# Moving an expert-weight transpose from TensorE and ScalarE to VectorE and the SP queue

## The reference: one attention layer and one retrieval FFN

```python
x = hidden_states                                   # (8, 2048, 256) float32
# attention: causal linear attention in chunks of 128, mixed with a fixed memory
sq, sk = elu(q) + 1, elu(k) + 1
A   = (sq_i @ sk_i.T) * tril                        # per chunk
out = (A @ v_i + sq_i @ S_kv) / (A.sum(-1) + sq_i @ z);  S_kv += sk_i.T @ v_i;  z += sk_i.sum()
x = x + layernorm((g * memory_output + (1 - g) * out) @ w_o.T)
# FFN: dense part and product-key experts (4 heads, 8 of 1024 experts each)
h = layernorm(x)
scores, indices = top_8(sx[:, None] + sy[None, :])  # two side scores per head, 1024 experts
w = silu((h @ down_embed[indices].T) * softmax(scores))
x = x + layernorm(silu(h @ W_up.T) @ W_down.T + w @ up_embed[indices])
```

## Time and profile before

| | |
|---|---|
| time, median of 3 runs | 3063.93 us (3062.81 to 3065.03) |
| time of the profiled execution | 3065.58 us |
| its span in the profile | 3063.8 us, so 1.8 us lie around it |
| PE busy | 3018.3 us, 99% |
| ACT busy | 2625.7 us, 86% |
| DVE busy | 2174.2 us, 71% |
| POOL busy | 1822.3 us, 59% |
| share of the chain of waits on PE | 96% |
| DMA: software queue (POOL's), hardware queue (SP's) | 36.5% and 4.3% of the 16 engines' span |

### The profile page before, as it was taken

The page is one execution under the profiler, slowest core; times in us unless marked ns, Lnnn a source line. Parts: engine busy times, 40 slices in busy tenths (PEclk is TensorE's granted clock), DMA queues, the critical chain, the costliest instruction groups (busy, mean ns, idle before and its releaser), DMA issues.

```text
span 3063.8 us, 48516 instructions
## 1 busy us (share of the span) xinstructions
PE 3018.3 (99%) x16506; PEld 2460.5 (80%) x16506; DVE 2174.2 (71%) x5644; ACT 2625.7 (86%) x4114; POOL 1822.3 (59%) x2455
## 2 busy tenths in 40 slices
PE   6999999999999999999999999999999999999997
PEld 5788888888888888888888888888888888888886
DVE  4767767776776777777677767767777776777774
ACT  3888888888888888888888888888888888888885
POOL 2665566566556656655665665566566556656653
PEclk8999999999999999999999999999999999999999
DMA  3344344334434433443443344344344434434443
GB/s 91 72 86 80 76 82 83 75 77 86 80 76 81 84 74 77 86 80 76 82 83 74 77 85 80 76 82 84 73 78 85 80 76 82 84 73 78 85 76 71
DMA packets 96201, 244.17 MB, mean 80 GB/s; under 512 B 8659, under 2 KB 46548, under 8 KB 95956
## 3 DMA queue, kind: packets, MB, share of 16 engines
q0 software_dynamic: 53248, 201.34, 36.5%
q1 hardware_dynamic: 42708, 39.73, 4.3%
HBM read 22.94 MB, written 16.78 MB: 13 GB/s over the span
## 4 chain that ended last, share of the span: by engine, by line
PE 96%; DMA 1%; issue 1%; POOL 0%; ACT 0%; SPq 0%; DVE 0%; POOLq 0%; DVEq 0%
PE banks L510 84%; PE banks L559 4%; PE banks L583 2%; PE banks L515 2%; PE banks L545 2%; PE banks L587 2%; PE banks L547 1%; DMA wexp<-wexp 1%; DMA sums<-in_L_ffn_keys_dram 0%; SPq L344 0%; POOL sums L400 0%; PE banks L494 0%; PE banks L501 0%; PE banks L479 0%; POOL rstd L386 0%
## 5 line engine op out<-in xcount | busy, mean ns | idle before, releaser
L400 POOL TENSOR_TENSOR sums<-scores 128x1024 f32<-128x1024 f32 x512 | 1076.7, 2218 | 389.6 <-ACT scores L632 389.6
L510 PEld LDWEIGHTS banks<-xn2T,wupT 128*128 128x128 f32 x4096 | 477.3, 192 | 9.2 <-DVE state L841 2.7
L510 PE MATMUL banks<-deT,xn2T 128*128 128x512 f32 x1024 | 481.3, 592 | 0.0
L510 PE MATMUL banks<-xn2T,wupT 128*128 128x128 f32 x4096 | 478.2, 275 | 1.9 <-DVE state L841 1.9
L510 PE MATMUL banks<-wdownT,hT 128*128 128x256 f32 x2048 | 465.3, 380 | 0.0
L510 PE MATMUL banks<-ue,gT 128*128 128x256 f32 x2048 | 462.9, 379 | 0.0
L510 PEld LDWEIGHTS banks<-wdownT,hT 128*128 128x128 f32 x2048 | 390.9, 191 | 53.9 <-issue 0.5
L510 PEld LDWEIGHTS banks<-ue,gT 128*128 128x128 f32 x2048 | 389.1, 190 | 53.8 <-issue 0.5
L386 POOL TENSOR_TENSOR rstd<-var_eps,minus_half 128x1 f32<-128x1 f32 x512 | 330.0, 702 | 60.7 <-DVE var_eps L823 42.3
L412 POOL TENSOR_TENSOR cprob<-cmask,cdif 128x112 f32<-128x112 f32 x128 | 65.9, 515 | 408.7 <-DVE cmask L746 408.7
L510 PEld LDWEIGHTS banks<-deT,xn2T 128*128 128x128 f32 x1024 | 184.7, 190 | 129.5 <-issue 122.9
(11 more groups left out here) (140 smaller groups left out, 7288.7 us busy)
## 6 DMA issues: line engine op xcount, KB each, us to landing
wexp<-wexp POOLq DMA_DIRECT2D x128, 1024.0 KB, 7.9
wexp<-wexp POOLq DMA_DIRECT2D x128, 512.0 KB, 4.8
x_in<-_attn_hidden_states_dram SPq DMA_DIRECT2D x128, 128.0 KB, 2.1
out_dram<-x_out SPq DMA_DIRECT2D x128, 128.0 KB, 1.7
wexp<-in_L_ffn_W_up_dram SPq DMA_DIRECT2D x1, 1024.0 KB, 8.2
prob<-in_L_ffn_down_embed_dram SPq DMA_DIRECT2D x1, 1024.0 KB, 10.7
ue<-in_L_ffn_up_embed_dram SPq DMA_DIRECT2D x1, 1024.0 KB, 12.9
wexp<-in_L_ffn_W_down_dram SPq DMA_DIRECT2D x1, 1024.0 KB, 12.6
```

The lines of the kernel that those rows point to most:

```text
L400: return nc.gpsimd.tensor_tensor(sums[:, k, :, :], scores[:, k, 0:XIN].unsqueeze(2).broadcast_to([P, XIN, NKEYS]), scores[:, HEADS + k, :] ...
L510: last = nc.tensor.matmul(out, lhs(c), rhs(c), start=(start and c == 0), stop=(stop and c == chunks - 1))
```

## The change

The transpose of the summed expert weights is done another way. DVE runs one `transpose` over the 128 x 1024 matrix, which turns each 32 x 32 block in place, into a new buffer `w_blocks`. The blocks are then in the wrong partitions, and SP moves them: 16 transfers for each tile, one for each pair of partition groups (i, j). Each has 32 partitions, 8 chunks and 32 elements, which is 256 pieces of 128 bytes, 32 KB in all. PE's eight transposes, ACT's two copies and the two PSUM banks go. Both semaphores on `gT` are replaced by two counters (even and odd tiles) that PE waits on, and DVE waits for the moves of the previous tile before it overwrites `w_blocks`.

The pipeline has nine steps of age in place of eight, `x_mid` has eight slots in place of four, and the order of the lines is new in every engine's body. Among these moves, DVE's `bn_stats` of `x_in` is now done for `t[0]`, in the step in which SP issues that tile's load.

```diff
-        STAGES = 8
+        STAGES = 9
-        x_mid = sb("x_mid", [P, SLOTS, D])
+    MID_SLOTS = 8
+        x_mid = sb("x_mid", [P, MID_SLOTS, D])
+        w_blocks = sb("w_blocks", [P, EXPERTS])
+        w_blocks_of = w_blocks[:, :].rearrange("p (c j q) -> p c j q", j=P // BLOCK, q=BLOCK)
+        def moved(eng, t):
+            if t >= 0:
+                eng.wait_ge(s_expert_weights_blocks_moved[t % 2], 16 * (P // BLOCK) ** 2 * (t // 2 + 1))
 # SP
-                if t[7] is not None:
-                    sp.wait_ge(s_x_out_ready, t[7] + 1)
+                if t[8] is not None:
+                    sp.wait_ge(s_x_out_ready, t[8] + 1)
...
+                if t[6] is not None:
+                    sp.wait_ge(s_expert_weights_blocks_turned, t[6] + 1)
+                    for i in range(P // BLOCK):
+                        for j in range(P // BLOCK):
+                            sp.dma_start(gT[j * BLOCK:(j + 1) * BLOCK, t[6] % 2, :, i * BLOCK:(i + 1) * BLOCK],
+                                         w_blocks_of[i * BLOCK:(i + 1) * BLOCK, :, j, :]).then_inc(s_expert_weights_blocks_moved[t[6] % 2], 16)
                 if t[0] is not None:
                     wait(sp, s_x_loaded, 16 * t[0])
...
 # PE
-                if t[5] is not None:
-                    pe.wait_ge(s_heads_summed, 16 * (t[5] + 1))
-                    for k in range(4):
-                        e = k
-                        last = nc.tensor.transpose(g_ps[0][:, k * P:(k + 1) * P], wexp[:, HEADS - 1, e * P:(e + 1) * P], ident[:, :])
-                    last.then_inc(s_expert_weights_T_0_in_psum, 1)
...
+                if t[7] is not None:
+                    moved(pe, t[7])
+                    product(y_ps, EC, lambda c: gT[:, t[7] % 2, c, :], lambda c: ue[:, c, :], start=False).then_inc(s_y_in_psum, 1)
 # ACT
-                    nc.scalar.copy(flat(gT[:, t[5] % 2, 0:4, :]), g_ps[0][:, :]).then_inc(s_expert_weights_T_0_ready, 1)
-                    nc.scalar.copy(flat(gT[:, t[5] % 2, 4:8, :]), g_ps[1][:, :]).then_inc(s_expert_weights_T_1_ready, 1)
+                    wait(act, s_expert_weights_blocks_turned, t[5])
 # DVE
+                if t[6] is not None:
+                    dve.wait_ge(s_heads_summed, 16 * (t[6] + 1))
+                    moved(dve, t[6] - 1)
+                    nc.vector.transpose(w_blocks[:, :], wexp[:, HEADS - 1, :]).then_inc(s_expert_weights_blocks_turned, 1)
-                if t[1] is not None:
-                    dve.wait_ge(s_x_loaded, 16 * (t[1] + 1))
-                    nc.vector.bn_stats(stats[:, LN_X, t[1] % 2, :], x_in[:, t[1] % SLOTS, :]).then_inc(s_x_stats, 1)
+                if t[0] is not None:
+                    dve.wait_ge(s_x_loaded, 16 * (t[0] + 1))
+                    if not steady:
+                        wait(dve, s_xn1_ready, t[0] - 1)
+                    nc.vector.bn_stats(stats[:, LN_X, t[0] % 2, :], x_in[:, t[0] % SLOTS, :]).then_inc(s_x_stats, 1)
```

More of the change, by code:

```diff
@@ L270, in sandwich_kernel @@
         s_head_3_weights_ready = sem("head_3_weights_ready")
+        s_expert_weights_blocks_moved = [sem(f"expert_weights_blocks_moved_{n}") for n in range(2)]
         s_state_zero = sem("state_zeroed")
@@ L524, in body @@
                 if t[3] is not None:
[L525 to L545, removed]
                     for c in range(DC):
@@ L589, in body @@
-                if t[3] is not None:
-                    wait(pe, s_xn1T_ready, t[3] + 2, TILES)
-                    pe.wait_ge(s_xn2_ready, t[3] + 1)
-                    turn(t_ps, xn2).then_inc(s_xn2T_in_psum, 1)
-                if t[2] is not None:
-                    pe.wait_ge(s_xn1T_ready, t[2] + 1)
-                    wait(pe, s_hidden_1_ready, t[2] - 1)
-                    for side, w in enumerate((wqT, wkT)):
-                        for ec in range(DC):
-                            col = (side * DC + ec) * P
-                            last = product(qk_ps[:, col:col + P], DC, lambda c: w[:, c, ec * P:(ec + 1) * P], lambda c: xn1T[:, c, :])
-                    last.then_inc(s_qk_in_psum, 1)
+                    pe.wait_ge(s_hidden_1_ready, t[6] + 1)
@@ L775, in body @@
                                                    ALU.mult, ALU.mult).then_inc(s_head_2_weighed, 1)
[L776 to L779 removed]
+                if t[2] is not None:
+                    dve.wait_ge(s_x_rstd, t[2] + 1)
+                    normed(xn1[:, :], x_in[:, t[2] % SLOTS, :], LN_X, t[2] % 2).then_inc(s_xn1_ready, 1)
+                if t[8] is not None:
+                    dve.wait_ge(s_y_rstd, t[8] + 1)
+                    wait(dve, s_x_stored, 16 * t[8])
+                    nc.vector.scalar_tensor_tensor(x_out[:, :], y_sb[:, 0:D], rstd[:, LN_Y, t[8] % 2:t[8] % 2 + 1], x_mid[:, t[8] % MID_SLOTS, :],
+                                                   ALU.mult, ALU.add).then_inc(s_x_out_ready, 1)
+                if t[5] is not None:
                     dve.wait_ge(s_head_3_prob_ready, t[5] + 1)
@@ new lines, in body @@
+                    for k in range(HEADS):
+                        last = nc.vector.max(best[:, k, :], cand[:, k, :])
+                    last.then_inc(s_best_ready, 1)
+                if t[0] is not None:
+                    dve.wait_ge(s_x_loaded, 16 * (t[0] + 1))
+                    if not steady:
+                        wait(dve, s_xn1_ready, t[0] - 1)
+                    nc.vector.bn_stats(stats[:, LN_X, t[0] % 2, :], x_in[:, t[0] % SLOTS, :]).then_inc(s_x_stats, 1)
+                if t[4] is not None:
+                    dve.wait_ge(s_down_1_in_psum, t[4] + 1)
+                    nc.vector.tensor_copy(last_down[:, t[4] % 2:t[4] % 2 + 1], d_ps[1][:, HALF - 1:]).then_inc(s_last_down_ready, 1)
```

352 lines of the change are left out of this document (176 added, 176 removed).

## The result

| | before | after |
|---|---|---|
| time, median | 3063.99 us (4 runs) | 4362.8 us (4 runs, 4360.12 to 4364.9) |
| ratio | | 1.4238, 95% interval 1.4217 to 1.4259 |
| span of the profiled execution | 3063.8 us | 4363.2 us |
| PE, DVE, ACT, POOL busy | 99, 71, 86, 59% | 74, 53, 58, 44% |

The forecast was 3925 us with a range of 3350 to 4750. Sign and mechanism came out as predicted; the step is 33.8 us where the forecast had 30.3. The measured time lies inside the range, but outside the central band of the prediction (3700 to 4310 us, a step of 28.5 to 33.5).

What follows compares the result with a forecast made beforehand. PE, busy 99%, was taken to bound the kernel; afterwards a loop of 16.2 + 1.2 + 8.2 + 2.1 us plus 2.6 contention makes 30.3 us steps: 3065.6 + 854 + 5 = 3925 us, range 3350 to 4750.

Steps and rivals of the forecast that it cites:

- PE without the transposes, 22.43 us a step: On PE, dropping two groups of four transposes at 0.44 us each takes a step's work from 23.31 to 22.43 us.
- A loop through the load of `x_in` sets the step: DVE transpose, sixteen SP issues, x_in load and DVE leg close a loop: 27.7 us undisturbed, 30.3 with contention.
- Rival 1: PE stays the bound and the kernel gets faster because SP issues transfers within SBUF cheaply; 2958 us, chance 8%.
- DVE leg 16.2 us: On DVE, from bn_stats to the next transpose, including sig's wait for ACT's exp; 14.2 us by work alone.
- Sixteen issues at 0.51, 8.2 us: On SP's queue, block transfers priced like setup loads of 256 pieces; 6.2 us as lower end, 9.0 as upper.
- Contention 2.6 us: In the DMA engines, the pair accumulate delays the landing of x_in by 0 to 5.8 us; 2.6 taken.
- Rival 2: The loop binds but accumulates don't disturb it: step 27.7 us, 3607 us, 20%; with cheaper issues 3363 us, another 6%.
- Pieces at 20 ns, hidden: In the DMA engines, 256 small pieces per engine and tile take 5.1 us, hidden behind 8.2 us of issuing.
- Rival 3: Small pieces are dear, at 49 ns each in the DMA engines: step 38.1 us, time 4876 us, chance 17%.
- TensorE's clock, 0: PE busy for 74% of a step may lose clock; cost put at 0, up to 2 us a step as bound.
- Rival 4: PE falls to half clock for good and is the bound again at 44.9 us; 5706 us, chance 4%.
- Ends of the run, 5 us: Steps outside the loop's 122 and the last tile's uncovered transpose and transfers add 5 us to the whole run.

Runs made afterwards that it cites:

- run 1: The changed kernel with SP's load of x_in issued ahead of the sixteen block transfers; 2995.6 us, ratio to the kernel before 0.9775.
- run 2: The changed kernel with DVE's bn_stats of x_in moved from the end of a step to just before bn_aggr of the next; 3853.8 us.
- run 3: The changed kernel with only eight of the sixteen block transfers issued, half of gT left at zero; 3900.5 us.
- run 4: The changed kernel with the pair accumulate cut to 128 of its 1024 columns, all sixteen block transfers kept; 3973.1 us.
- run 5: The changed kernel with two of eight chunks in each of the sixteen block transfers, 64 pieces in place of 256; 4269.1 us.
- run 7: The changed kernel with each of the sixteen 32 KB transfers made of 32 pieces of 1 KB, gT not the transpose; 4249.7 us.
- runs 5 to 8: Besides run 5 and run 7, the changed kernel with transfers spanning 128 partitions, 4366.8 us, and with transfers reading HBM in place of w_blocks, 4276.5 us.

## Why the prediction was right, and where its size was off

- **PE without the transposes, 22.43 us a step.** Right for PE's own work: 22.44 in the step shown of run 1, with PE busy throughout. The mean there is 22.69, because PE waits for `gT` in part of the steps. The prediction gave PE "nearly a step" for that, which is a little too much in run 1.
- **A loop through the load of `x_in` sets the step.** Right. The wait stands at `bn_stats` in 122 steps, as counted. Run 1 opened the loop and run 2 shortened it, and the step went as its sum says (in run 2 within 0.3 us); in runs 3 and 4 the sum with the unchanged leg of 16.25 us holds within 0.1 us. Rival 1 is out: an issue costs 0.60 us and not 0.24 to 0.36. Of the signs, DVE's idle time is 12.1 us a step where I wrote 5 to 10, in the right place.
- **DVE leg 16.2 us, with a wait of `sig` for the exp in it.** Right: 16.25, with 1.64 us of that wait. The last exp on ACT starts 11.6 us behind `bn_stats` and `sig` 12.2, close to the 11.9 and 0.3 of the sum. By work alone (14.2) it would have been too short.
- **Transpose 1.2 us.** Right: 1.24.
- **Sixteen issues at 0.51, 8.2 us.** This is the term that was mis-sized. They cost 0.65 to 0.66 apart, 10.5 us, above the upper end of 9.0. The rows behind the 0.51 and the 0.56 were of the setup, and the lower end of 0.39 came from a store. The cost per issue is right in kind: it did not go by pieces (run 5).
- **Contention 2.6 us, between 0 and 5.8.** The size was near, 3.3 to 3.5, and that was luck: it was a choice a little under the middle of the bounds, and the place was wrong. I had put it on the landing of `x_in`, for which I expected over 4 us and which stayed at 2.3. It fell on SP's issues under the accumulate, and only where the load comes earlier (run 3) does it fall on the landing, 7.2 us. Rival 2, no contention, is out.
- **Pieces at 20 ns, hidden.** They cost 12.7 ns and are hidden. Rival 3 is out as a mechanism. Its band of steps, from 33.5 us up, is where the result fell, but by dear issues and not by dear pieces. Of the two statements of the Trainium skill (DMA: Bandwidth & Descriptors), the trace is nearer to the one that spares copies within SBUF (Why small descriptors are slow) than to the read-modify-write below 512 B (Specifications): the 128-byte pieces show no penalty that the step would feel, and run 7 with pieces of 1 KB gained only 113 us. They are not free by the byte, though. A 1 KB piece took 45 ns in run 7 (18.0% of 3 us, 192 packets), and eight small ones take 102. The 40 ns that the prediction tried for the first statement came from no row.
- **TensorE's clock, 0.** The prediction read rows 1 as full clock from the first slice on; that slice shows 8 and only the others 9, which changes no term. After the change it did fall, to 0.85 over a step. PE's up products took 368 ns where they had taken 275, but the leg on DVE came out as computed, so it cost next to nothing. Rival 4 is out: PE is 2% of the chain.
- **Ends of the run, 5 us.** About right for the kernel after: with the mean step it is 4363.2 - 3063.8 - 122 x (33.88 - 23.31) = 10 us. In run 1 it is 2999.8 - (3063.8 - 128 x 0.62) = 15 us. There the first tile is finished at 147.2 us in place of 123.9, and from the last load to the last `x_out` it takes 149.4 in place of 139.4.

In sum: 2.3 us for issues, 0.9 for contention and 0.3 for the other terms make 3.5 us a step, 122 x 3.5 = 427 us of the 438 us by which 3925 fell short. These misses all have the same sign, and the range held because it reached far up for rival 3, whose mechanism did not occur.

## What to carry to other kernels

An issuing queue that is idle for 97% of a step (0.77 us of 23.31 here) has a price as soon as something is put ahead of the one thing that others wait for. Before adding transfers, ask what stands behind them, and follow it round: if its consumer must run before the next batch can start, the whole chain is a lower limit of the step, whatever the totals of each engine say. The same transfers behind the load cost 0.26 us a step, by PE's waits for `gT`, and the transpose on DVE and SP is then worth 2.2%. Price an issue from the steady state, per transfer and not per byte, and look at what the other DMA queue does at that moment.

## What the runs showed of the hardware

- In the steady part a block issue of SP takes 0.59 to 0.62 us (medians), with 32, 64 or 256 pieces, 32 or 128 partitions, source in SBUF or HBM (after, runs 5 to 8), and a load behind them 0.60. Why a load of 256 pieces takes 0.47 in the setup, and the load of `x_in` 0.43 behind a store, stays open.
- While an accumulating DMA of 1 MB runs, an issue of SP takes up to 1.6 us with 64 pieces a transfer (run 5) and 1.5 with 32 (run 7), and the hardware queue moves 90 packets in 5 us in place of 1638. With the accumulate cut to an eighth this is gone from the step shown (run 4). A load of 128 KB issued under it lands in 7.2 us in place of 2.3 (run 3). What in the engines or the descriptor path does this was not separated.
- 128-byte pieces within SBUF took 12.7 ns of a DMA engine each (after), pieces of 1 KB 45 ns (run 7).
- A 32 x 32 block transpose of 128 x 1024 float32 on DVE took 1.24 us.
